# A graph-attention and FFN kernel: the edge mask by scatters into device tables, and weight lows on VectorE

## The reference

```
h = layernorm(x)
q, k, v = h @ wq.T + bq, h @ wk.T + bk, h @ wv.T + bv
q2, k2, v2 = (t @ wi.T + bi for t, wi, bi in (q,wiq,biq), (k,wik,bik), (v,wiv,biv))   # 16 heads of 64
w = softplus(edge_type_weights)                       # 4 weights
mask = full((384, 384), -inf)
mask = mask.at[src, dst].set(w[edge_type - 1])        # 6528 edges, a later edge overwrites an earlier
mask[i, i] = w[3] where the diagonal has no edge
attn = softmax(q2 @ k2.T * scale + mask)
x = x + (attn @ v2) @ wo.T + bo
x = x + ffn(layernorm(x))        # int8-like rounding of weights and activations: gate, up, down (352 wide)
```

## Time and profile before

| | us |
|---|---|
| median of 3 runs | 385.93 (385.56 to 387.04) |
| the profiled execution | 387.39 |
| its span | 385.7 |
| TensorE busy | 357.1 (93%) |
| VectorE busy | 257.4 (67%) |
| ScalarE busy | 177.9 (46%) |
| GpSimd busy | 198.6 (52%) |

### The profile page before, as it was taken

The page is one execution under the profiler, slowest core; times in us unless marked ns, Lnnn a source line. Parts: engine busy times, 40 slices in busy tenths (PEclk is TensorE's granted clock), DMA queues, the critical chain, the costliest instruction groups (busy, mean ns, idle before and its releaser), DMA issues.

```text
span 385.7 us, 6449 instructions
## 1 busy us (share of the span) xinstructions
PE 357.1 (93%) x2145; PEld 308.4 (80%) x2145; DVE 257.4 (67%) x685; ACT 177.9 (46%) x331; POOL 198.6 (52%) x288
## 2 busy tenths in 40 slices
PE   4799979999999999999999699999999998995973
PEld 4799967877777777999999599999999877872631
DVE  5855688657587783634418277897897883677366
ACT  2633335654711221334338366876776774316420
POOL 6776565987353244487890726446446665000003
PEclk9999989999999999999999979999999999996978
DMA  7584325553132211333441312032033233000004
GB/s 277 177 296 145 109 75 192 188 187 116 50 109 65 100 55 54 109 110 109 140 132 57 109 56 73 39 109 87 24 111 92 74 109 109 2 0 1 2 0 163
DMA packets 12922, 38.66 MB, mean 100 GB/s; under 512 B 1768, under 2 KB 3040, under 8 KB 12896
## 3 DMA queue, kind: packets, MB, share of 16 engines
q1 hardware_dynamic: 12048, 37.63, 29.3%
q10 hardware_dynamic: 848, 0.70, 0.6%
HBM read 36.74 MB, written 1.58 MB: 99 GB/s over the span
## 4 chain that ended last, share of the span: by engine, by line
PE 83%; DVE 9%; ACT 3%; DMA 2%; POOL 1%; issue 1%; SPq 0%; DVEq 0%; ACTq 0%
PE PS L685 59%; PE PS L780 7%; PE PS L832 4%; PE PS L820 3%; PE PS L808 3%; PE PS L668 2%; PE PS L963 2%; DMA X<-in_x 1%; DVE stats L987 1%; DMA stage<-in_weights 1%; DVE X L1303 1%; DVE V L1300 1%; ACT PT L478 1%; POOL ring L392 1%; PE PS L974 1%
## 5 line engine op out<-in xcount | busy, mean ns | idle before, releaser
L392 POOL TENSOR_TENSOR ring<-stage,ring 128x256 fp32r<-128x256 f32 x208 | 155.3, 778 | 96.2 <-ACT ring L468 96.0
L685 PE MATMUL PS<-XT,ring 128*128 128x384 f32 x576 | 119.7, 352 | 0.5 <-DVE XT L1019 0.5
L685 PEld LDWEIGHTS PS<-XT,ring 128*128 128x128 f32 x576 | 101.6, 191 | 4.2 <-issue 0.7
L468 ACT ACTIVATE ring<-stage 128x1024 fp32r<-128x1024 f32 x52 | 54.4, 1058 | 23.2 <-DMA stage<-in_weights 22.9
L685 PE MATMUL PS<-AT,ring 128*128 128x384 f32 x192 | 38.0, 356 | 3.4 <-DVE Q L1136 3.4
L685 PEld LDWEIGHTS PS<-AT,ring 128*128 128x128 f32 x192 | 35.8, 202 | 4.9 <-issue 4.9
L560 ACT ACTIVATE scratch<-scratch,smx 128x384 f32<-128x384 f32 x48 | 28.9, 604 | 17.1 <-DVE smx L1149 17.1
L685 PE MATMUL PS<-QT,ring 128*128 128x384 f32 x192 | 35.6, 339 | 0.0
L685 PE MATMUL PS<-ring,AT 128*128 128x512 f32 x144 | 34.5, 394 | 0.0
L780 PE MATMUL PS<-scratch 128*128 128x384 bf16 x156 | 34.4, 330 | 0.0
L685 PEld LDWEIGHTS PS<-QT,ring 128*128 128x128 f32 x192 | 33.1, 188 | 0.3 <-issue 0.2
(11 more groups left out here) (186 smaller groups left out, 519.6 us busy)
## 6 DMA issues: line engine op xcount, KB each, us to landing
stage<-in_weights SPq DMA_DIRECT2D x56, 512.0 KB, 3.3
V<-in_w_gate_up SPq DMA_DIRECT2D x4, 512.0 KB, 3.8
X<-in_x SPq DMA_DIRECT2D x3, 512.0 KB, 4.9
out<-X SPq DMA_DIRECT2D x6, 256.0 KB, 2.1
scratch<-in_w_gate_up SPq DMA_DIRECT2D x2, 512.0 KB, 3.9
V<-in_w_down SPq DMA_DIRECT2D x5, 176.0 KB, 3.7
scratch<-in_w_down SPq DMA_DIRECT2D x3, 176.0 KB, 3.4
scratch<-in_bias_o ACTq DMA_DIRECT2D x1, 512.0 KB, 3.9
```

The source lines that it names most:

```text
L392: ins = pool.tensor_tensor(ring[1][:, slot, piece], stage[:, slot % STAGE, piece], ring[0][:, slot, piece].bitcast(F32), ALU.subtract)
L468: act.activation(ring[0][:, slot, :], stage[:, slot % STAGE, :], ACT.Copy).then_inc(w_high, 1)
L685: ins = pe.matmul(outs, lhs[a], rhs[b], start=start and n == 0, stop=stop and n == 2, skip_group_check=True)
```

## The change

- The one-hot products go, on VectorE and on TensorE. Instead there are three tables of 384 x 384 floats in device memory (`codes`). SP fills them with zeros from a block of SBUF that GpSimd has cleared, between the loads of chunks 5 and 6. VectorE makes, behind the duplicate tests, the place of each edge in a table (key, or a number out of range for an overwritten edge). GpSimd scatters 51 columns of 128 codes with indirect DMAs, 17 per table, in turn over the tables; each waits until the one before it in its table has landed. Codes of a later table are 16 times as large.
- When the scatters have landed (and the FFN steps and bias additions no longer need the scratch area), GpSimd reads the three tables back. VectorE waits for them behind the fourth k tile, adds them and the diagonal, and makes the mask in the later part of the k stage.
- The lows of chunks 10 to 31 are made by VectorE, in one operation of 1024 columns each; GpSimd keeps chunks 0 to 9 and 32 to 55. The bias additions move to VectorE, into the q stage.
- FFN steps 0 to 2 come behind tiles 4 to 6 in place of 5 to 7.

The diff, cut to its core:

```diff
+GROUPS = 13
+LISTS = 3
+PER_LIST = E // P // LISTS
...
+            next_chunk(5)
+            sp.wait_ge(blank_ready, 1)
+            for b in range(LISTS):
+                sp.dma_start(codes[b].rearrange("(m p n) -> p m n", m=NT, p=P), blank.to_broadcast([P, NT, N])
+                             ).then_inc(codes_blank[b], 16)
+            for c in range(6, 10):
...
+            pool.memset(scratch[:, 3 * C:3 * C + N], 0.0).then_inc(blank_ready, 1)
...
-            pool.wait_ge(code_ready, 1)
-            pool.tensor_tensor(ecol[:, VAL, :], ecol[:, TYP, :], code_e[:, :].bitcast(F32), ALU.mult
-                               ).then_inc(cols_ready, 1)
+            for b in range(LISTS):
+                part_b = slice(b * PER_LIST, (b + 1) * PER_LIST)
+                ins = pool.tensor_scalar(ecol[:, VAL, part_b], ecol[:, TYP, part_b], 16.0 ** (b + 1), 0.0,
+                                         ALU.mult, ALU.add)
+            ins.then_inc(cols_ready, 1)
             def low(c, slot):
                 pool.wait_ge(w_high, c + 1)
                                              ring[0][:, slot, piece].bitcast(F32), ALU.subtract)
                 ins.then_inc(w_low, 1)
-            for c in range(CIV):
+            for c in range(CIV + 2):
                 low(c, c % RING)
-            pool.wait_ge(bc_in, 16)
-            pool.wait_ge(y_ready, NT)
-            for c in range(CIV, CIV + 8):
-                low(c, c % RING)
-                if c < CIV + 2 * NT:
-                    m, hf = (c - CIV) // 2, c % 2
-                    cs = slice(hf * HC, (hf + 1) * HC)
-                    pool.tensor_tensor(X[:, m, cs], X[:, m, cs], bo_bc[:, cs], ALU.add).then_inc(bo_added, 1)
-            with pool.Fori(0, 4) as i:
-                for j in range(4):
-                    low(4 * i + (CQ + j), j)
+            pool.wait_ge(place_ready, 1)
+            for i in range(PER_LIST):
+                for b in range(LISTS):
+                    t = b * PER_LIST + i
+                    if i:
+                        pool.wait_ge(scattered[b], 16 * i)
+                    else:
+                        pool.wait_ge(codes_blank[b], 16)
+                    pool.indirect_dma_start(codes[b].rearrange("(n a) -> n a", a=1),
+                                            bass.IndirectOffsetOnAxis(ap=place[:, t:t + 1], axis=0),
+                                            ecol[:, VAL, t:t + 1], None, bounds_check=N * N - 1, oob_is_err=False
+                                            ).then_inc(scattered[b], 16)
+            pool.wait_ge(bo_added, 2 * NT)
+            pool.wait_ge(ffn_full, 8)
+            for b, area in enumerate((SM[0], SM[1], mask)):
+                pool.wait_ge(scattered[b], 16 * PER_LIST)
+                pool.dma_start(area, codes[b].rearrange("(m p n) -> p m n", m=NT, p=P)).then_inc(code_back, 16)
+            pool.wait_ge(w_low, CPAIR)
             for c in range(CPAIR, CPAIR + 4):
...
-            pe.wait_ge(diag_ready, 1)
-            pe.wait_ge(acc_free, NT)
-            for s in range(NT):
-                pe.matmul(PS[:, ACC + s, 0:N], diag[:, :], wide[:, (2 - s) * P:(5 - s) * P], start=True, stop=False,
-                          skip_group_check=True)
-            def edge(e, slot):
-                pe.wait_ge(oh_ready, e + 1)
-                for s in range(NT):
-                    ins = pe.matmul(PS[:, ACC + s, 0:N], onehot[:, slot, 0, s * P:(s + 1) * P],
-                                    onehot[:, slot, 1, :], start=False, stop=False, skip_group_check=True)
-                ins.then_inc(oh_used, 1)
-            with pe.Fori(0, 2) as i:
-                for j in range(4):
-                    first = 2 * sum(ONE_HOT) * i + (sum(ONE_HOT) * (j // 2) + ONE_HOT[0] * (j % 2))
-                    begin(4 * i + (CQ + j), 4 * i + (8 + j))
-                    if j < 2:
-                        pe.wait_ge(acc_free, (NT + 1, 2 * NT)[j])
-                    finish(part(j, j % 2, XT, range(KT), lambda k: edge(first + k, k) if k < ONE_HOT[j % 2] else None))
-            for s in range(NT):
-                ins = pe.matmul(PS[:, ACC + s, 0:N], wide[:, 0:P], wide[:, 0:N], start=False, stop=True,
-                                skip_group_check=True)
-            ins.then_inc(code_full, 1)
+            pe.wait_ge(acc_free, NT + 1)
+            project(CQ, 8, 0, XT)
+            pe.wait_ge(acc_free, 2 * NT)
+            for c in range(CQ + 1, CK):
+                project(c, c - CQ + 8, c % RING, XT)
...
+            def low(c):
+                dve.wait_ge(w_high, c + 1)
+                dve.tensor_tensor(ring[1][:, c % RING, :], stage[:, c % STAGE, :], ring[0][:, c % RING, :].bitcast(F32),
+                                  ALU.subtract).then_inc(w_low, 1)
...
             for s in range(8):
                 tile_low(s, s, s % 2, AT, BIAS_V + s)
                 for g in (2 * s, 2 * s + 1):
-                    if g < 13:
+                    if g < GROUPS:
                         once(g)
-                if s > 4:
-                    ffn_step(s - 5)
-            dve.wait_ge(key_used, 13)
-            used = slice(0, 4 * 13)
-            chain.step(dve.scalar_tensor_tensor(ecol[:, VAL, used], dup[:, used], 0.0, ecol[:, VAL, used],
-                                                ALU.is_equal, ALU.mult))
+                if s == 6:
+                    dve.wait_ge(key_used, GROUPS)
+                    used = slice(0, LISTS * PER_LIST)
+                    dve.scalar_tensor_tensor(place[:, used], dup[:, used], 2.0 ** 20, ecol[:, KEY, used], ALU.mult, ALU.add
+                                             ).then_inc(place_ready, 1)
+                if 3 < s < 7:
+                    ffn_step(s - 4)
+            dve.wait_ge(w_low, CIV + 2)
             for s in range(3, 8):
+                low(CIV + s - 1)
                 ffn_step(s)
-            dve.wait_ge(ffn_full, 8)
-            dve.wait_ge(bo_added, 2 * NT)
-            def one_hot(first, before, n):
-                for s in range(n):
-                    e = first + s
-                    dve.wait_ge(oh_used, before + (min(s, ONE_HOT[1] - 1) + 1 + EPS))
-                    dve.tensor_scalar(onehot[:, s, 0, :], iota[:, :], ecol[:, SRC, bass.ds(e, 1)],
-                                      ecol[:, VAL, bass.ds(e, 1)], ALU.is_equal, ALU.mult)
-                    dve.tensor_scalar(onehot[:, s, 1, :], iota[:, :], ecol[:, DST, bass.ds(e, 1)],
-                                      None, ALU.is_equal).then_inc(oh_ready, 1)
-            def q_tile(s, b):
-                tile_low(s + 8, s, b, QT, s + BIAS_Q)
-            ROUND = sum(ONE_HOT)
-            one_hot(0, -EPS, ONE_HOT[0])
-            with dve.Fori(0, 3) as i:
-                one_hot(ROUND * i + ONE_HOT[0], ROUND * i, ONE_HOT[1])
-                q_tile(2 * i, 0)
-                one_hot(ROUND * i + ROUND, ROUND * i + ONE_HOT[0], ONE_HOT[0])
-                q_tile(2 * i + 1, 1)
-            one_hot(3 * ROUND + ONE_HOT[0], 3 * ROUND, ONE_HOT[1])
-            q_tile(6, 0)
-            q_tile(7, 1)
+            for c in range(CIV + 7, CIV + 10):
+                low(c)
+            dve.wait_ge(bc_in, 16)
+            for s in range(8):
+                low(CQ + 2 + s)
+                if s < 2 * NT:
+                    m, cs = s // 2, slice(s % 2 * HC, (s % 2 + 1) * HC)
+                    dve.tensor_tensor(X[:, m, cs], X[:, m, cs], bo_bc[:, cs], ALU.add).then_inc(bo_added, 1)
+                tile_low(s + 8, s, s % 2, QT, s + BIAS_Q)
...
-            code = PS[:, ACC:ACC + NT, 0:N]
-            dve.wait_ge(code_full, 1)
+            def k_tile(s):
+                if CK + 2 + s < CPAIR:
+                    low(CK + 2 + s)
+                tile_low(s + 16, s, s % 2, AT, s + BIAS_K)
+            for s in range(4):
+                k_tile(s)
+            dve.wait_ge(code_back, 16 * LISTS)
+            chain.step(dve.tensor_tensor(mask, mask, SM[0], ALU.add))
+            k_tile(4)
+            chain.step(dve.tensor_tensor(mask, mask, SM[1], ALU.add))
+            for m in range(NT):
+                own = mask[:, m, m * P:(m + 1) * P]
+                chain.link(dve.tensor_tensor(own, own, diag[:, :], ALU.add))
+            chain.join()
+            k_tile(5)
             kind = SM[0].bitcast(I32)
-            chain.step(dve.tensor_scalar(kind, code.bitcast(I32), 21, 3, ALU.logical_shift_right, ALU.bitwise_and))
-            chain.step(dve.tensor_scalar(mask, code, 0.0, NO_EDGE, ALU.is_equal, ALU.mult))
-            base = chain.n
-            with dve.Fori(0, 4) as w:
-                chain.n = 2 * w + base
-                tile_low(2 * w + 16, 2 * w, 0, AT, 2 * w + BIAS_K)
-                chain.step(dve.tensor_scalar(SM[1], kind, kinds[:, bass.ds(w, 1)], ew[:, 5, bass.ds(w, 1)],
-                                             ALU.is_equal, ALU.mult))
-                tile_low(2 * w + 17, 2 * w + 1, 1, AT, 2 * w + (BIAS_K + 1))
```

(14 more changed lines are left out.)

49 lines of the change are left out of this document (17 added, 32 removed).

## The result

| | us, each execution | median | ratio to before, 95% interval |
|---|---|---|---|
| before | 383.70, 385.56, 385.93, 387.04 | 385.75 | |
| changed | 361.37, 363.43, 365.44, 366.78 | 364.44 | 0.9447 [0.9362, 0.9533] |

The change takes 21.3 us off; 27.5 were forecast.

The account below looks back on a forecast made before the run. TensorE, busy 93% of the span, was taken as the bound nearly everywhere. Span 385.7 - 27.0 - 1.5 + 1.0 + 0 = 358.2, median 358.4 us; own range 353.5 to 361, and 353.5 to 383 with B and D.

Parts of the forecast that it names:

- the case in which the scatters are hidden: The main forecast: scatters end before VectorE needs the tables; 358.4 us, range 353.5 to 361, chance 0.52.
- rival B: Scatters partly uncovered: 5.7 us a round, 1.9 per scatter, ending 12.2 us late; 370.6 us, chance 0.20.
- the prediction's own signs: Profile checks: last scatter landing before 142 us; no TensorE idle in the k stage; idle at its seventh chunk means wrong.
- The q stage, -27.0: Without one-hot matmuls the q stage holds what the k stage holds: 60.4 - 33.4 = 27.0 us gained.
- V and inner V, -1.5: 16 to 96 us: earlier FFN steps remove TensorE's idle and slow projection; between 0.5 and 4.3 gained, 1.5 taken.
- by hand, with the old durations: V stage, VectorE's queue re-timed: step 0 ends at 47.3, step 1 at 54.1, places 57.0, step 2 at 61.2.
- The 2.2 us of lateness at 59 us: TensorE's third FFN transposition, due at 59.0, waits for VectorE's step 2 until 61.2: 2.2 us come back.
- Scatters hidden, 0: 51 scatters from 57.0 at 1.5 us each end at 133.5, limit 141.7: 8 us in hand, nothing lost.
- The limit (tables landed by 149.7): K stage: tables must land by 149.7, before VectorE's work for the seventh chunk at 152.9; scatters end by 141.7.
- The end of the k stage, +1.0: Three mask passes behind the last tile make the first Q part 0.9 us late, 0 to 2; 1.0 lost.
- C: Rival: scatters become the bound, kernel slower, from 2.2 us per scatter; 410 us at 2.67; chance 0.18.
- D: Rival: VectorE becomes the bound, lows stretching from 1.20 to 2.1 us beside GpSimd's issues; 363 us, chance 0.10.

Follow-up runs that it names:

- edge-free kernel: Kernel before without VectorE's one-hot products and TensorE's edge matmuls, so the mask leaves edges out: 359.38 to 365.5 us, ratio 0.9334.
- nine scatters: Changed kernel issuing only the first 9 of 51 scatters, 3 per table, leaving out most edges: 358.75 to 363.11 us, ratio 0.9358.
- the later wait: Changed kernel with VectorE's table wait behind six k tiles, not four, and first pair's lows between the last mask passes: ratios 0.934 and 0.9316.
- the loop: TensorE's q stage as a loop of two passes over four chunks: on the changed kernel 0.9407; with the table wait also moved 0.9302 and 0.9322.
- narrow lows: Changed kernel with VectorE's last 14 of 22 weight lows made for 8 of 1024 columns only: 361.33 us, ratio 0.936.
- two tables: Changed kernel with two of three tables scattered, 34 scatters, the third left blank: 361.22 us, ratio 0.9368.

## Why the prediction was right, and where its sizes were off

The kernel is faster, as forecast. But 364.4 us lies above 361, the upper end of the case in which the scatters are hidden, and between it and rival B's 370.6. Two of the prediction's own signs also came: the last landing was at about 143.3 us, not before 142, and TensorE was idle at the seventh k chunk. That the profiled spans differ by 26.4, so near 27.5, is in part luck: 2.1 us more were gained before the q stage, against 1.3 less in the q and k stages and 1.9 more lost behind them.

**The q stage, -27.0: right, -25.5 to -25.7.** The edge-free kernel measured it without any scatter. The missing 1.3 us are two idles of 0.5 (152.12 and 101.42) and 0.3 of work.

**V and inner V, -1.5: too small, -3.6, and -3.3 by itself.** The step that failed is "by hand, with the old durations": the step of 4.16 us had run beside GpSimd's bias addition and low and took 3.1 at its new place (the three together 10.1, not 12.5), and the place computation took 0.21, not the 1.3 of its similar row. The 2.2 us of lateness at 59 us that I subtracted did not come; 0.79 did.

**Scatters hidden, 0: the mechanism and the limit right, the margin not.** The limit (tables landed by 149.7) was within 1.3 us of the truth: tables at 148.92 cost 0.51, so the edge is at 148.4, earlier because the seventh chunk was due at 151.6, not 152.9. The estimate of 1.5 us a scatter measured 1.63, and the last landing came at about 143.3, not 133.5 (the last wait of GpSimd for a scatter ends then). The third read-back, issued at 143.34, landed 5.6 us later, where I had 8 us for all three; without that second error, which helped, the wait would by this sum have been 2.4 us longer. I took the landing, 4.1 us a round (4.2 measured), as what sets a round, with the issues inside it; but three issues are 4.4 themselves, and the round was 4.9. That is the step that failed: an issue priced at 0.8 us, "one GpSimd piece", took 1.46 with what comes between two and what VectorE holds, so three of them were not well inside the landing. So 8.2 us in hand became -0.5 in the best execution and -3.65 in another. That is rival B's mechanism, with waits of 0.51 and 3.65 us where B had 12.2, and it is a good part of why the median gained 21.3 where the profiled spans differ by 26.4: nine scatters gained 5.8 us on 51, and a late execution pays the wait and then a lower clock behind it, which none of my cases had priced. (The profiled executions are also the longest of before and the shortest of after.)

From the fixed 2.0 us of a DMA in the Trainium skill (DMA: Bandwidth & Descriptors, "Anatomy of one DMA — SWDGE (gpsimd) path") I had estimated 0.7 us per scatter; the rows differ, with 3.0 us to landing in place of 2.0 and GpSimd busy for 0.97 of each.

**The end of the k stage, +1.0: too small, +2.9.** A pass behind the last tile takes 1.18 + 1.78 us or more where I had 1.01 + 1.35. All three take 9.3 us, from 162.17 to 171.49, in place of 7.1: with a start 0.3 earlier that is the missing 1.9. TensorE shows it as 0.84 + 1.96 us of idle. The addition takes 1.36 at 148.92 and 1.78 right behind the pass whose result it reads; in the kernel with nine scatters too. Why was not tested.

**The rivals.** C's held issues exist, 0.19 us per scatter on the mean (1161 against 970 ns) where I had taken 0.12, but the whole scatter came to 1.63 and C began at 2.2. D did not come: lows at 1.22 us, not 2.1.

The version that beats both kernels is the changed one with the later wait: 0.934 and 0.9316 on two chips, with the loop 0.9302 and 0.9322, some 26 us under before.

## What to carry to other kernels

Work that is moved to an idle engine is hidden only up to the instruction that waits for it: work out that deadline, and put the wait as late as the work behind it allows before counting any margin. Where two limits of a repeated round lie close together, the round can cost more than either (here 4.9 us, with 4.2 and 4.4). Waits of 3.65 and 2.95 us cost TensorE 1.6 and 2.7 us more in clock here, so a margin that one execution shows as just enough can be a loss in the median.

## What the runs showed of the hardware that I had not expected

- An indirect scatter of 128 single elements holds GpSimd 0.97 us with 0.30 to the next one, and 3.0 us from issue to landing in the median; begun inside a VectorE operation with both inputs in SBUF, it ends 0.83 to 0.85 us after that one (and so takes up to 1.99).
- An idle of 1.96 us left 18 matmuls at 3.39 us; one of 2.69 too (3.39, narrow lows); 2.93 made it 4.95 (two tables), 2.95 made it 6.07. The length of the idle alone does not order the loss: at the later stall 24 matmuls took 7.03 us behind 3.19 us of idle (later wait, granted clock 0.59) and 5.98 behind 3.36 (changed kernel, 0.72).
- In one profiled execution ScalarE was idle for 27.5 us with its input ready for most of it, and TensorE and VectorE waited for it, beside scatters that ran at full pace. Why is open.
